# First cross attention: the scores of two heads at once on two 64-row tiles, from one masked copy of the keys

## The reference, cut to what matters

```python
Q = (query @ Wq.T + bq).reshape(B, Lq, H, D)          # B 8, Lq 256, H 16, D 8
K = (key_value @ Wk.T + bk).reshape(B, Lkv, H, D)      # Lkv 256
V = (key_value @ Wv.T + bv).reshape(B, Lkv, H, D)
scores = einsum('bqhd,bkhd->bhqk', Q, K) / sqrt(D)
scores = where(mask[:, None, None, :] == 0, -inf, scores)
probs = softmax(scores, axis=-1)
context = einsum('bhqk,bkhd->bqhd', probs, V).reshape(B, Lq, E)
return context @ Wo.T + bo
```

## Time and profile before

| what | us |
|---|---|
| median of 3 runs | 1981.62 (1978.43 to 1983.26) |
| the profiled execution, its own time | 1982.75 |
| its span, first to last instruction | 1980.9 |
| PE busy / PE weight loads busy | 1417.6 / 753.8 |
| DVE / ACT / POOL busy | 1440.6 / 1137.4 / 1200.4 |
| the score matmuls of this stage (L833), busy | 137.3 |
| the masked key copies (L971), 128 of 493 ns | about 63 |
| the second stage's score pairs (L846), 512 weight loads and matmuls | 1551.9 to 1874.7 |

### The profile page before, as it was taken

How to read it: one execution, slowest core, us unless ns; L and a number is a source line. 1 busy time by engine, 2 the same in 40 slices (tenths; PEclk the granted TensorE clock), 3 DMA queues, 4 the chain that set the end, 5 groups by cost and what they waited for, 6 DMA issues and landing times. The chain is left out here.

```text
span 1980.9 us, 23714 instructions
## 1 busy us (share of the span) xinstructions
PE 1417.6 (72%) x6931; PEld 753.8 (38%) x6931; DVE 1440.6 (73%) x2510; ACT 1137.4 (57%) x2515; POOL 1200.4 (61%) x759
## 2 busy tenths in 40 slices
PE   3899899995755556655566565556535899999968
PEld 2777577773311112211112121111101566666523
DVE  3666488885508988989898888999984566666734
ACT  2543688884636555555555555555533677777720
POOL 2000356560029999999999999999993243444400
PEclk8999899996567767777677776777866899999978
DMA  3000000000034323343322432333213000000000
GB/s 101 1 1 1 1 2 1 0 1 1 0 132 175 120 111 150 126 153 150 139 97 108 172 150 106 150 150 135 95 70 86 1 1 1 1 0 1 1 0 22
DMA packets 51970, 134.40 MB, mean 68 GB/s; under 512 B 19076, under 2 KB 28568, under 8 KB 39448
## 3 DMA queue, kind: packets, MB, share of 16 engines
q1 hardware_dynamic: 49112, 130.78, 17.4%
q10 hardware_dynamic: 2496, 2.36, 0.4%
q0 software_dynamic: 256, 0.01, 0.0%
HBM read 114.26 MB, written 18.87 MB: 67 GB/s over the span
## 5 line engine op out<-in xcount | busy, mean ns | idle before, releaser
L1470 POOL TENSOR_TENSOR ma_hs<-ma_dtuR,ma_Bt 128x1024 f32<-128x1024 f32 x256 | 596.4, 2353 | 7.1 <-DMA ma_dtuR<-ma_dtu_d 6.9
L1629 ACT ACTIVATE ps<-ma_dtR,ma_A 128x512 f32<-128x512 f32 x512 | 332.7, 682 | 361.2 <-DVE ma_hs L1763 221.3
L786 POOL TENSOR_TENSOR x_pr<-x_pr,x_rec 128x512 f32<-128x512 f32 x256 | 267.5, 1045 | 352.7 <-DVE x_rec L1035 352.7
L1547 PE MATMUL ps<-ma_hs,ma_fold 128*32 128x512 f32 x1024 | 198.4, 915 | 293.8 <-POOL ma_hs L1478 237.3
L1757 DVE TENSOR_TENSOR_SCAN ps<-ps,ma_hs 128x1024 f32<-128x1024 f32 x144 | 329.1, 2286 | 5.7 <-POOL ma_hs L1470 4.5
L1757 DVE TENSOR_TENSOR_SCAN ma_hs<-ps,ma_hs 128x1024 f32<-128x1024 f32 x112 | 255.9, 2284 | 47.1 <-POOL ma_hs L1470 38.6
L1001 ACT ACTIVATE x_pr<-x_sm,x_mx 128x256 f32<-128x256 f32 x512 | 254.5, 500 | 52.5 <-DVE x_mx L1026 52.0
L1478 POOL TENSOR_TENSOR ma_hs<-ma_hs,ma_Ct 128x1024 f32<-128x1024 f32 x112 | 262.9, 2348 | 0.4 <-DVE ma_hs L1757 0.4
L1547 PEld LDWEIGHTS ps<-ma_hs,ma_fold 128*32 128x32 f32 x1024 | 37.9, 144 | 422.4 <-issue 337.7
L1514 PE MATMUL ps<-ma_hn,ma_w_tap 128*128 128x512 f32 (+3 forms) x256 | 147.4, 741 | 59.7 <-ACT ma_hn L1647 47.8
L1763 DVE TENSOR_TENSOR ma_hs<-ps,ma_Ct 128x1024 f32<-128x1024 f32 x144 | 176.3, 1225 | 5.0
(11 more groups left out here) (308 smaller groups left out, 2466.8 us busy)
## 6 DMA issues: line engine op xcount, KB each, us to landing
ma_dtuR<-ma_dtu_d SPq DMA_DIRECT2D x32, 1024.0 KB, 7.0
ma_dtR<-ma_dt_d SPq DMA_DIRECT2D x32, 1024.0 KB, 8.9
ma_Bt<-ma_bc_d SPq DMA_DIRECT2D x16, 1024.0 KB, 5.0
ma_Ct<-ma_bc_d SPq DMA_DIRECT2D x16, 1024.0 KB, 6.9
ma_dtu_d<-ma_dtu SPq DMA_DIRECT2D x32, 256.0 KB, 2.0
ma_dt_d<-ma_dt SPq DMA_DIRECT2D x32, 256.0 KB, 2.3
ma_cwb<-in_L_attn_conv_w_dram SPq DMA_DIRECT2D x4, 512.0 KB
x_m<-in_mask_BxSxS_fk_dram SPq DMA_DIRECT2D x1, 2048.0 KB, 11.2
```

The lines of the kernel that those rows point to most:

```text
L786: pool.tensor_tensor(pr[:, r, :, :], pr[:, r, :, :], rec[:, r, :].unsqueeze(2).broadcast_to([P, 2, L]), ALU.mult).then_inc(pr_done, 1)
L1470: pool.tensor_tensor(hs[:, k % SLOTS, :, :], dtuR[:, unit(f, h), q, :].unsqueeze(1).broadcast_to([P, 2, CH]), rows(Bt, k), ALU.mult).then_ ...
L1547: mm = pe.matmul(c.ps[q * E32:(q + 1) * E32, Y[h], :], fold[:, :], hs[:, (k0 + q) % SLOTS, a, :], start=False, stop=(j % 2 == 1 and a == 1 ...
L1629: e = act.activation(c.ps[:, 2 * (k % 2) + a, :], dtR[:, unit(f, h), q, :], ACT.Exp, scale=A[:, (f // QUARTERS) % 2, h, q, no:no + 1])
```

## The change: two heads from one matmul group

`small` now uses `score_pair` too. One masked copy of the keys carries two heads: head a on its 8 partitions in the lower half (partitions 0 to 63), head a + 8 in the upper half. PE computes the two heads on the two 64-row tiles of the array: each matmul reads 64 partitions of `q` and of `km`, and the two results go to bank 0 and bank 1. ACT makes 8 copies for a batch instead of 16, at even steps. The order of the heads changes (`head`) so that steps n and n + 1 are such a pair and four steps still fill the four 32-partition parts of the weigh result. The mask `mine` becomes two columns for a pair; DVE adds them once at the stage's start (`member`). The pair waits for `max_done` of both heads of the pair before (`b * NH + n`), where the single score of head n waited for that of head n - 2.

```diff
--- before.py
+++ after.py
@@ -702,7 +702,7 @@
 
     def head(n):
 
-        return 4 * (n % 4) + n // 4 if small else n
+        return n // 4 + 4 * (n // 2 % 2) + 8 * (n % 2) if small else n
 
     with Stage(c, name) as s:
         cb = s.sb("cb", [P, L])
@@ -722,12 +722,13 @@
             k = s.sb("k", [P, 2, L])
             v = s.sb("v", [P, 2, 2, 4, 160])
             mr = s.sb("mr", [P, 2, L])
-            km = s.sb("km", [P, 2, NH, L])
-            mine = s.sb("mine", [P, NH])
+            km = s.sb("km", [P, 2, NH // 2, L])
+            mine = s.sb("mine", [P, NH // 2, 2])
+            member = s.sb("member", [P, NH // 2])
         (consts, ctx_in, proj, evac, neg_done, km_done, scores, s_free, shifted, max_done,
-         exp_done, rec_done, pr_done, turned, pT_done, pv, oT_done, out_done, x_done) = (s.sem(n) for n in (
+         exp_done, rec_done, pr_done, turned, pT_done, pv, oT_done, out_done, x_done, member_done) = (s.sem(n) for n in (
             "consts ctx_in proj evac neg_done km_done scores s_free shifted max_done exp_done "
-            "rec_done pr_done turned pT_done pv oT_done out_done x_done").split())
+            "rec_done pr_done turned pT_done pv oT_done out_done x_done member_done").split())
 
 
         flat = pr[:, :, :, :].rearrange("p a t k -> p (a t k)")
@@ -769,15 +770,14 @@
             def _(pool):
                 if small:
                     pool.memset(v[:, :, :, :], 0.0).then_inc(consts, 1)
-                    pool.memset(mine[:, :], 1.0).then_inc(consts, 1)
+                    pool.memset(mine[:, :, :], 1.0).then_inc(consts, 1)
                     pool.wait_ge(consts, 2)
 
-                    pool.affine_select(out=mine[:, :], in_=mine[:, :], compare_op=ALU.is_ge, fill=0.0, base=0,
-                                       pattern=[[-D, NH]], channel_multiplier=1).then_inc(consts, 1)
+                    pool.affine_select(out=mine[:, :, :], in_=mine[:, :, :], compare_op=ALU.is_ge, fill=0.0, base=0,
+                                       pattern=[[-D, NH // 2], [-64, 2]], channel_multiplier=1).then_inc(consts, 1)
                     pool.wait_ge(consts, 3)
-                    pool.affine_select(out=mine[:, :], in_=mine[:, :], compare_op=ALU.is_ge, fill=0.0, base=D - 1,
-                                       pattern=[[D, NH]], channel_multiplier=-1).then_inc(consts, 1)
-
+                    pool.affine_select(out=mine[:, :, :], in_=mine[:, :, :], compare_op=ALU.is_ge, fill=0.0, base=D - 1,
+                                       pattern=[[D, NH // 2], [64, 2]], channel_multiplier=-1).then_inc(consts, 1)
 
                 def body(b, p, fresh, first, last):
                     for n in range(NH):
@@ -821,30 +821,20 @@
                                            start=True, stop=True)
                     mm.then_inc(proj, 1)
 
-                def score(b, p, n, first):
-                    bank = c.ps[:, n % 2, :]
+                def score_pair(b, p, n, first):
+
                     if n == 0:
                         pe.wait_ge(evac, b * NP + NQK)
                     if n >= 2 or not first:
-                        pe.wait_ge(max_done, b * NH + n - 1)
-                    h = head(n)
-                    pe.wait_ge(km_done, b * NH + n + 1)
-                    for t in range(2):
-                        mm = pe.matmul(bank[:, t * L:(t + 1) * L], q[:, p, 0, t * P:(t + 1) * P], km[:, p, h, :],
-                                       start=True, stop=True)
-                    mm.then_inc(scores, 1)
-
-                def score_pair(b, p, n, first):
-
-                    if n == 0:
-                        pe.wait_ge(evac, b * NP + NQK)
-                    if n >= 2 or not first:
-                        pe.wait_ge(s_free, b * NH + n)
+                        pe.wait_ge(max_done if small else s_free, b * NH + n)
+                    if small:
+                        pe.wait_ge(km_done, b * (NH // 2) + n // 2 + 1)
                     for t in range(2):
                         for r in range(2):
                             row = slice(64 * r, 64 * r + 64)
-                            mm = pe.matmul(c.ps[:, r, t * L:(t + 1) * L], q[row, p, n // 2, t * P:(t + 1) * P],
-                                           k[row, p, n // 2, :], start=True, stop=True)
+                            queries = q[row, p, 0 if small else n // 2, t * P:(t + 1) * P]
+                            keys = km[row, p, n // 2, :] if small else k[row, p, n // 2, :]
+                            mm = pe.matmul(c.ps[:, r, t * L:(t + 1) * L], queries, keys, start=True, stop=True)
                             if t == 1:
                                 mm.then_inc(scores, 1)
 
@@ -906,9 +896,7 @@
 
                 def body(b, p, fresh, first, last):
                     for n in range(NH):
-                        if small:
-                            score(b, p, n, first)
-                        elif n % 2 == 0:
+                        if n % 2 == 0:
                             score_pair(b, p, n, first)
                         if not last:
                             for a in units(n):
@@ -965,17 +953,18 @@
                 act.activation(cb[:, :], c.cT[:, 0:L], ACT.Copy).then_inc(ctx_in, 1)
                 if small:
                     act.wait_ge(consts, 4)
-                def keys_of_head(b, p, n):
-
-                    h = head(n)
-                    act.activation(km[:, p, h, :], k[:, p, :], ACT.Copy, scale=mine[:, h:h + 1]).then_inc(km_done, 1)
+                def keys_of_pair(b, p, n):
+
+                    a = head(n)
+                    act.activation(km[:, p, n // 2, :], k[:, p, :], ACT.Copy, scale=member[:, a:a + 1]).then_inc(km_done, 1)
 
                 for n in range(NP):
                     evacuate(0, 0, n, True, False)
                 if small:
                     act.wait_ge(evac, NQK)
-                    for n in range(4):
-                        keys_of_head(0, 0, n)
+                    act.wait_ge(member_done, 1)
+                    for n in range(0, 4, 2):
+                        keys_of_pair(0, 0, n)
 
                 def step(b, p, n, first):
                     if masked_rows:
@@ -987,12 +976,12 @@
                         if not last:
                             for a in units(n):
                                 evacuate(b + 1, 1 - p, a, False, first)
-                        if small and n + 4 < NH:
-                            keys_of_head(b, p, n + 4)
-                        elif small and not last:
+                        if small and n % 2 == 0 and n + 4 < NH:
+                            keys_of_pair(b, p, n + 4)
+                        elif small and n % 2 == 0 and not last:
                             if n + 4 == NH:
                                 act.wait_ge(evac, b * NP + NP + NQK)
-                            keys_of_head(b + 1, 1 - p, n + 4 - NH)
+                            keys_of_pair(b + 1, 1 - p, n + 4 - NH)
                         step(b, p, n, first)
                         if n >= RP or not first:
                             act.wait_ge(turned, b * NH + n - RP + 1)
@@ -1056,6 +1045,7 @@
 
                 if small:
                     dve.wait_ge(consts, 4)
+                    dve.tensor_reduce(member[:, :], mine[:, :, :], AX.X, ALU.add).then_inc(member_done, 1)
                 else:
                     dve.wait_ge(c.mask1_in, 16)
```

## The result

| | us |
|---|---|
| before, median of 4 runs | 1982.44 (1978.43 to 1985.97) |
| after, median of 4 runs | 2000.19 (1998.91 to 2001.24) |
| ratio after / before | 1.0094, 95% interval 1.0077 to 1.0111 |
| span of the profiled execution, before / after | 1980.9 / 1999.2 |
| stage, first projection to the end of the last sum into x, before / after | 232.9 / 252.6 |

The change makes the kernel 0.94% slower. The forecast was 1985 with a range of 1978 to 1994: the sign of its likeliest case was right, its size (3.4 us) was a fifth of what came (17.8), and the range missed.

What follows compares the result with a forecast made beforehand. A loop of DVE copy, weigh, score and DVE maximum was taken to bound the stage. A batch goes from 27.84 to 28.27 us, eight batches +3.4 us, on the 1981.62 median 1985.0; range 1978 to 1994.

Steps and rivals of the forecast that it cites:

- likeliest case: Whole kernel: no change or the forecast's few us of loss, +3.4 us; chance 0.57.
- What bounds before: Cross attention stage: loop of DVE copy, weigh, score, DVE maximum closes once in four heads, 6.55 us a group.
- PE's side of the pair: PE: eight overlapping loads in 0.73 us, next turn at 1.06, 0.17 ahead; weigh pair 3.24 us, under 3.34.
- rival A: PE bounds the weigh pairs at 3.48 us, 1988.4; a 1.36 us hand-off likewise gives 1996; chance 0.26.
- C: Rival: the pair's tiles do not overlap in this stage, eight loads take 1.52 us, 2034 us; chance 0.03.
- B: Rival: hand-off shorter (scores reach DVE within 0.76 us) or overlapped, 1970 or 1962 us; chance 0.08.
- the weigh chain or the drains: Trace sign on PE: what q evacuations over 28.6 us apart would point to; 28.3 was forecast.
- The mechanism of the hand-off: PE to DVE: a pair fills both banks, waits for both earlier maxima; DVE idles every second head.
- Its size: Hand-off: 0.05 us to the loads, 1.17 to DVE's start (bounds 0.76 and 1.36); 3.34 us a pair.
- The clock: Granted clock in the stage: under 1.00 would add to all times; the second stage still shows 1.00.
- The other edits: ACT's 8 saved key copies a batch worth nothing, at most 3.2 us; DVE's start reduction hidden.

Runs made afterwards that it cites:

- b_four_banks: The kernel before (single scores, 16 key copies) with four score banks instead of two and the projections sharing one bank; 1993.08 us, 1.0065 of before.
- a_dve_order: The changed kernel with DVE doing both maxima of a pair first, then the two reciprocals and copies; 1968.96 us, 0.9948 of before.
- b_wait_both: The kernel before with two single scores issued back to back, both waiting for the two maxima of the two heads before; 2023.63 us, 1.0221 of before.
- a_two_inc: The changed kernel with a second semaphore increment on DVE between the wait for the scores and each maximum; 2012.98 us, 1.0160 of before.
- a_km_first: The changed kernel with a pair's two waits swapped, key copy first and maxima last; 2002.29 us, 1.0114 of before.
- a_km_twice: The changed kernel with every masked key copy made twice, so ACT again makes 16 a batch; 2001.16 us, 1.0105 of before.

## Why the prediction missed

By its own steps:
- *What bounds before.* Not contradicted: b_four_banks leaves the group at 6.56 us, though PE's own work is close under it.
- *PE's side of the pair.* Right: 0.74 for eight loads, 1.07 to the turn, 0.17 ahead, turns of 0.42 behind a gap; the weigh pair at 3.25 when PE bounds it (a_dve_order). Rivals A (by PE) and C fall, and B with them, since DVE gets the first head after 1.36 us and not 0.76. By the prediction's own sign, evacuations over 28.6 us apart meant "the weigh chain or the drains"; they came at 29.97 with PE idle 0.59 us behind the weigh, so the sign pointed at the wrong term.
- *The mechanism of the hand-off.* Right: both maxima must be done, DVE waits every second head (b_wait_both, a_dve_order).
- *Its size.* Wrong, and this is the step that failed. "From the pair's loads to DVE's start" was taken as 1.17 us "since its matmuls have the same shape". But in the second stage the one who waits is another: a plain operation, with its wait on it. The maximum here is a custom operation behind a semaphore increment. It measured 1.36, at times 1.41, which is the earlier trace rows of the same DVE operation after a single score, and stood in the prediction as the upper bound. Of the 0.19 us the increment is 0.09 (a_two_inc); the rest is open. The start of the loads, forecast at 0.05, was 0.06 outside the hardware loop and 0.12 to 0.13 in it (a_km_first). In the loop 0.12 + 1.36 + 1.36 + 0.77 = 3.61 us for seven pairs and 4.65 measured for the one with projections (4.89 forecast) make 29.9 us a batch, as measured: +2.1 in place of +0.43. After the first half batch this came to 14.3 us.
- *The clock.* Not counted. The prediction named a granted clock under 1.00 as what would add, and took comfort from the second stage, which holds 1.00; but that stage shows PE busy 38.6 of 40 us, the changed one 143.2 of 180 (260 to 440 us). In the middle it stayed 1.00 all the same. At the start PE ran at 1.2 GHz in both kernels, and in the changed one 15 us longer. Five pairs from 224.34 to 247.44 took 23.1 us; at the distances of the next batch, 4 x 3.53 + 4.64 = 18.8. Later batches lose 1.6 to 2.15 us each, so half a batch about 1.0, and about 4.4 of the first half batch's 5.4 us are the clock's, an estimate.
- *The other edits.* Right: the copies are worth nothing (a_km_twice).

The price of a late hand-off was in the prediction's working (1996 with 1.36, given under rival A), and the range stopped at 1994. Worked out anew: pairs of 3.53 and one of 4.65 give +12.2 us in eight batches, the later starts in the loop (7 x 0.08 in four batches) 2.2, and the clock about 4.4, together some 2000 us.

## What to carry to other kernels

A stage that halves an engine's work by taking two buffers at once gives up its double buffering; price the hand-off, and give the consumer other work for it (DVE's order) or a second set of buffers, before counting the engine's saving. Read the latency of a hand-off from a row with the same consumer and the same form of wait, not only the same producer. Where several waits stand ahead of an instruction their order can be worth 0.06 us either way, so read it in the loop and outside it before settling it.

## What the runs showed of the hardware

- A semaphore increment on DVE between a wait and the operation costs 0.09 us when DVE is waiting and nothing when it is not (a_two_inc: 1.36 to 1.45 us; 1.36 in the stream either way).
- Two waits ahead of PE's load, one long fulfilled and one late: inside the hardware loop the load came 0.12 to 0.13 us after the awaited event with the late wait first and 0.05 to 0.06 with it last; in the batches outside the loop 0.05 to 0.06 with it first and 0.11 to 0.12 with it last (after, a_dve_order, a_km_first, best_two). The reason is not shown.
- Of the two levels, 1.2 GHz lasted until 244.6 us in the changed kernel, where PE idles more at the start of the stage, and until 229.7 in the kernel before; with extra matmuls in the gaps 2.4 GHz held from 224.3 and 230.6. In one profile (a_two_inc) the clock fell twice in mid-stage, for some 4 and 7 us, each time behind an idle stretch of PE's loads of 2.13 and 2.40 us, and held 1.00 behind a third of 2.15; in the changed kernel, where the longest there is 1.69, it held 1.00.
